# Routing of the last four token tiles at once, counts behind the first block, and destination columns rewritten in halves

## What is computed

```python
router_logits = x @ gate_w.T                         # 16 experts
topk_w, topk_idx = jax.lax.top_k(softmax(router_logits), 4)
topk_w = topk_w / topk_w.sum(axis=-1, keepdims=True)
shared = _silu_mul(x @ shared_gate_up.T, 704) @ shared_down.T
shared = shared * sigmoid(x @ shared_gate_vec.T)
# for each expert: acc + (silu_mul(x @ w_gu.T) @ w_d.T) * combine weight
return shared + sparse
```

## Time and profile before

| | before |
|---|---|
| runs, median (lowest to highest) | 738.39 us (736.25 to 744.0) |
| the profiled execution, device time | 739.09 us |
| its span | 737.3 us |
| TensorE busy | 560.7 us (76%) |
| VectorE busy | 492.3 us (67%) |
| GpSimd busy | 344.7 us (47%) |
| ScalarE busy | 285.3 us (39%) |
| indirect transfers of the dispatch (L1280), busy | 65.2 us in 64 |

### The profile page before, as it was taken

How to read it: one execution, slowest core, us unless ns; L and a number is a source line. 1 busy time by engine, 2 the same in 40 slices (tenths; PEclk the granted TensorE clock), 3 DMA queues, 4 the chain that set the end, 5 groups by cost and what they waited for, 6 DMA issues and landing times. The chain is left out here.

```text
span 737.3 us, 14872 instructions
## 1 busy us (share of the span) xinstructions
PE 560.7 (76%) x4194; PEld 483.8 (66%) x4195; DVE 492.3 (67%) x1202; ACT 285.3 (39%) x692; POOL 344.7 (47%) x420
## 2 busy tenths in 40 slices
PE   4268898899864998878388989950389999999900
PEld 1146677777753887767266868840289999999900
DVE  0567888889860648474848687540567777777758
ACT  1244445554532644334133434320344444444400
POOL 1026576677653446656610766672024444444410
PEclk9698999999985999999669999985599999999955
DMA  9121212221002755261132366535484444443177
GB/s 303 68 72 37 65 46 72 71 64 43 28 1 82 221 160 175 71 202 43 43 89 82 135 196 201 182 134 172 110 256 132 131 129 130 129 129 115 67 288 307
DMA packets 66122, 91.82 MB, mean 125 GB/s; under 512 B 8544, under 2 KB 56480, under 8 KB 66080
## 3 DMA queue, kind: packets, MB, share of 16 engines
q1 hardware_dynamic: 56144, 69.79, 31.4%
q0 software_dynamic: 6912, 19.01, 7.1%
q10 hardware_dynamic: 3024, 2.50, 1.0%
HBM read 53.23 MB, written 35.95 MB: 121 GB/s over the span
## 5 line engine op out<-in xcount | busy, mean ns | idle before, releaser
L1623 POOL DMA_INDIRECT results<-yb,xe x80 | 77.0, 962 | 109.6 <-DVE yb L1706 106.9
L1280 POOL DMA_INDIRECT dispatched<-rows,slot x64 | 65.2, 1019 | 46.5 <-DVE slot L1372 27.1
L1755 PE MATMUL bank<-wgu_hi,xT_hi 128*128 x160 | 60.1, 375 | 3.2 <-DVE xT_lo L1687 3.2
L1739 PE MATMUL bank<-ident,xe 128*128 128x128 f32 x160 | 32.0, 284 | 37.8 <-DMA xe<-dispatched 37.3
L1700 DVE TENSOR_TENSOR e_hT_lo<-bank,e_hT_hi 128x256 fp32r<-128x256 f32 x80 | 34.0, 425 | 32.2 <-ACT e_hT_hi L1656 32.2
L980 DVE TENSOR_TENSOR a_lo<-act,a_hi 128x512 fp32r<-128x512 f32 x32 | 28.3, 885 | 39.6 <-ACT a_hi L946 39.2
L1755 PE MATMUL bank<-wgu_lo,xT_hi 128*128 x160 | 52.6, 329 | 0.0
L1755 PE MATMUL bank<-wgu_hi,xT_lo 128*128 x160 | 52.5, 328 | 0.0
L435 POOL TENSOR_TENSOR orms<-omse,neghalf 128x16 f32<-128x16 f32 x16 | 46.7, 2921 | 1.7 <-POOL omse L432 0.8
L1739 PEld LDWEIGHTS bank<-ident,xe 128*128 128x128 f32 x160 | 19.9, 145 | 39.9 <-DMA xe<-dispatched 38.1
L542 DVE TENSOR_TENSOR probs<-bank,causal 128x512 f32<-128x512 f32 x64 | 42.1, 683 | 4.8 <-PE bank L677 4.4
(11 more groups left out here) (235 smaller groups left out, 1920.0 us busy)
## 6 DMA issues: line engine op xcount, KB each, us to landing
dispatched<-fill SPq DMA_DIRECT2D x20, 520.0 KB, 6.8
xe<-dispatched SPq DMA_DIRECT2D x80, 130.0 KB, 2.3
trig<-t_trig SPq DMA_DIRECT2D x16, 512.0 KB, 3.5
stage<-expert_gu SPq DMA_DIRECT2D x16, 352.0 KB, 3.5
wgu_hi<-results SPq DMA_DIRECT2D x11, 512.0 KB, 7.9
xt<-L_attn_x SPq DMA_DIRECT2D x32, 128.0 KB, 3.5
wgu_lo<-results SPq DMA_DIRECT2D x5, 512.0 KB, 16.5
x_rows<-h_all SPq DMA_DIRECT2D x16, 128.0 KB, 2.0
```

The costliest lines, as they stand in the source:

```text
L1280: pool.indirect_dma_start(out=dram["dispatched"], out_offset=bass.IndirectOffsetOnAxis(ap=slot[:, k, t:t + 1], axis=0), in_=rows[:, t, :], ...
L1623: pool.indirect_dma_start(out=dram["results"], out_offset=bass.IndirectOffsetOnAxis(ap=xe[:, r, E:E + 1].bitcast(INT), axis=0), in_=yb[:, ...
L1739: tr = nc.tensor.transpose(t_bank[r % 2][:, k * P:k * P + P], xe[:, r, k * P:k * P + P], ident[:, :])
L1755: mm = nc.tensor.matmul(gu_bank[p][:, 0:GU], xT[xn_][:, p, k, :], wgu[wn][:, k, e, :], start=(k == 0 and i == 0), stop=(k == KB - 1 and i ...
```

## The change

`choose` handles tiles 12 to 15 in one set of operations of four times the width, at the very start, with the still unused `x4` as scratch; only the running count is made tile by tile. SyncE therefore waits for the third step of the chain before it loads `x4`. `count` moves behind `first_product` of block 0, and `bases` and `slots(0)` behind VectorE's block 0; the other slots and the three `low_down` follow. GpSimd rewrites the destination column in two halves of eight tiles, each waiting only for its own eight transfers of the round before, and waits in round k for k + 1 slot vectors.

```diff
@@ GpSimd
+            def number(k, half):
+                for t in range(half * HALF, half * HALF + HALF):
+                    wait(pool, s_sent[t], 16 * k)
+                cols = slice(half * HALF, half * HALF + HALF)
+                nc.gpsimd.tensor_copy(rows[:, cols, E:E + 1].bitcast(INT), dest[:, k, cols].unsqueeze(2)).then_inc(S["col"], 1)
+            pool.wait_ge(S["tab_in"], 64)
+            number(0, 0)
+            number(0, 1)
             for k in range(TOPK):
-                for t in range(NT):
-                    wait(pool, s_sent[t], 16 * k)
...
-                nc.gpsimd.tensor_copy(rows[:, :, E:E + 1].bitcast(INT), dest[:, k, :].unsqueeze(2)).then_inc(S["col"], 1)
-                pool.wait_ge(S["col"], k + 1)
-                pool.wait_ge(S["slots"], TOPK)
-                for t in range(NT):
...
+                for half in range(2):
+                    if k:
+                        number(k, half)
+                    pool.wait_ge(S["col"], 2 * k + half + 1)
+                    pool.wait_ge(S["slots"], k + 1)
+                    for t in range(half * HALF, half * HALF + HALF):
@@ VectorE
-            choose(NT - 4)
-            low_down(0)
-            low_down(1)
+            choose()
...
                 if g == 0 and b == 0:
-                    choose(NT - 2)
-                    choose(NT - 1)
+                    bases()
+                    slots(0)
+                    low_down(0)
                 elif g == 0 and b == 1:
+                    low_down(1)
                     low_down(2)
-                    bases()
-                elif g == 0 and b in (2, 3):
-                    slots(2 * b - 4)
-                    slots(2 * b - 3)
+                    slots(1)
+                elif g == 0 and b == 2:
+                    slots(2)
+                elif g == 0 and b == 3:
+                    slots(3)
@@ SyncE
+                if first:
+                    sp.wait_ge(S["chain"], 3)
@@ TensorE
-                pe.wait_ge(S["chain"], 5 * TPG)
+                pe.wait_ge(S["chain"], 4 + TPG)
...
-                    if isinstance(g, int) and g == 0 and b == 2:
+                    if isinstance(g, int) and g == 0 and b == 0:
                         count()
```

More of the change, by code:

```diff
@@ L1175, in shared_and_dispatch @@
         later, ones = sh[:, 0, 0:P], sh[:, 0, P:2 * P]
-        versus = sh[:, 1, :].rearrange("p (e x) -> p e x", x=NX)
+        versus = x4[:, :, :].rearrange("p t (e x) -> p t e x", x=NX)
         steps, tile_no = sb("steps", [P, NX]), sb("tile_no", [P, ETILES])
@@ L1269, in _ @@
             pool.wait_ge(s_filled, 16 * (ETILES // 4))
-            for k in range(TOPK):
-                for t in range(NT):
-                    wait(pool, s_sent[t], 16 * k)
-                if k == 0:
-                    pool.wait_ge(S["tab_in"], 64)
-                nc.gpsimd.tensor_copy(rows[:, :, E:E + 1].bitcast(INT), dest[:, k, :].unsqueeze(2)).then_inc(S["col"], 1)
-                pool.wait_ge(S["col"], k + 1)
-                pool.wait_ge(S["slots"], TOPK)
-                for t in range(NT):
-                    pool.indirect_dma_start(out=dram["dispatched"], out_offset=bass.IndirectOffsetOnAxis(ap=slot[:, k, t:t + 1], axis=0),
-                                            in_=rows[:, t, :], in_offset=None).then_inc(s_sent[t], 16)
+            HALF = NT // 2
+            def number(k, half):
[6 more added lines that the diff above has]
+            number(0, 1)
+            for k in range(TOPK):
+                for half in range(2):
[4 more added lines that the diff above has]
+                    for t in range(half * HALF, half * HALF + HALF):
+                        pool.indirect_dma_start(out=dram["dispatched"], out_offset=bass.IndirectOffsetOnAxis(ap=slot[:, k, t:t + 1], axis=0),
+                                                in_=rows[:, t, :], in_offset=None).then_inc(s_sent[t], 16)
             for t in range(NT):
@@ L1341, in flat, with choose @@
                 return x[:, :, :].rearrange("p t e -> p (t e)")
[L1343 to L1349, removed]
-                chain(nc.vector.tensor_tensor(before_tile[:, t + 1, :], before_tile[:, t, :], chosen[:, t, :], ALU.add))
+            def choose():
+                last = slice(NT - TPG, NT)
+                chain(nc.vector.tensor_tensor(versus[:, :, :, :], logits[:, last, 0:NX].unsqueeze(2).broadcast_to([P, TPG, NX, NX]),
+                                              logits[:, last, 0:NX].unsqueeze(3).broadcast_to([P, TPG, NX, NX]), ALU.subtract))
+                chain(nc.vector.scalar_tensor_tensor(versus[:, :, :, :], ebefore[:, :, :].unsqueeze(1).broadcast_to([P, TPG, NX, NX]), -TINY,
+                                                     versus[:, :, :, :], ALU.mult, ALU.is_lt))
+                chain(nc.vector.tensor_reduce(order[:, last, :], versus[:, :, :, :], AX.X, ALU.add))
+                chain(nc.vector.tensor_scalar(chosen[:, last, :], order[:, last, :], TOPK - 0.5, None, ALU.is_lt))
+                for t in range(NT - TPG, NT):
+                    chain(nc.vector.tensor_tensor(before_tile[:, t + 1, :], before_tile[:, t, :], chosen[:, t, :], ALU.add))
+                return done[0]
             def bases():
@@ L1459, in body @@
                             add_shared(g - 1, i, 1 - q)
-                    if isinstance(g, int) and g == 0 and b == 0:
-                        choose(NT - 3)
                     hidden(g, b)
```

## The result

| | before | after |
|---|---|---|
| runs, median (lowest to highest) | 739.03 us (736.25 to 744.0) | 720.29 us (715.64 to 728.84) |
| runs | 4 | 4 |

The ratio is 0.9733, with a 95% interval of 0.969 to 0.9776: 18.7 us less, where 721.5 us had been predicted. Ratios and intervals, here and in the experiments, leave out executions more than 1.5% above the fastest of their kernel; medians are those of all. The execution whose trace is read here is the slowest of the four, 728.84 us: its work ahead of the changed stage took 8.9 us longer than before's (the stage starts at 384.44 instead of 375.54), so times are given from the stage's start, as "+101.5". A second profile of the same kernel, from the experiments (`e9_change_again`, 720.62 us, stage from 374.35), has no such delay and is read beside it.

The account below looks back on a forecast made before the run. The scatter chain was taken to end the shared stage some 18 us after the compute chain; with compute ending at 493.5, the next stage starts 17.8 us earlier: 739.09 - 17.8 = 721.3, given as 721.5, range 718 to 727.

Parts of the forecast that it names:

- What bounds the kernel: Between shared and expert stage: GpSimd's scatters and the load behind them end some 18 us after compute and its stores.
- The start of the scatter: GpSimd's first scatter, waiting only for slots(0) behind block 0, starts at 391.0, 15.2 us earlier than before.
- The turns: GpSimd's column rewrites between scatters: six of 2.0 us (1.5 to 3.0) replace three of 5.0; last issue at 478.5.
- The shared ports: Each of GpSimd's six column copies could lose 0.75 us to a VectorE instruction, 4.5 in all, without moving the sum.
- The slack: At the stage's end: expert_d lands at 490.0, 5.4 us before the scatter chain would decide the end.
- Rival 1: Scatter chain still ends the stage last; with every second turn at its old 5.0 us, 725 us; chance 0.12.
- The compute chain: The shared expert's blocks up to VectorE's last operation: 0.3 us late from the load wait, ending at 493.5.
- the walk: Step-by-step timing of the first blocks: first expert load there at 396.9, ScalarE's split 0.8 us, hid(2) at 398.6.
- The sum: The next stage begins at 496.9 instead of 514.76, 17.8 us earlier, with the expert stage unchanged: 721.3, given as 721.5.
- Rival 2: Late staging: each of the first four expert loads holds ScalarE and VectorE 1.4 us longer, 727 us; chance 0.10.
- Rival 3: Nothing gained, as the next stage waits for something else at its start: 738 us; chance 0.04.
- Rival 4: TensorE's clock stays at 1.2 GHz for part of the expert loop; fifteen tiles give 751 us; chance 0.04.

Follow-up runs that it names:

- e9_change_again: The changed kernel itself, nothing altered, timed once more in the second set: 722.15 us, ratio 0.9785.
- e6_before_two_rounds: The kernel before with two of its four rounds of scatters left out, the combine reading the other two twice: 723.01 us, ratio 0.9796.
- e3_change: The changed kernel itself, nothing altered, timed beside its variants on another occasion: 786.92 us, ratio 1.063.
- e11_short_rows: The changed kernel with 64 more scatters, of 16-byte rows into a tensor of their own, ahead of its own scatters: 800.34 us in a single run.
- e4_down_first: The changed kernel with the first two low_down calls back ahead of block 0, as before the change: 786.18 us, ratio 1.0617.
- first and third sets: Two of four groups of kernels timed together, on different chips; the change took 786.92 us in the first, the variant nearest to it 785.15 in the third.
- second and fourth sets: The other two groups of kernels timed together; the change took 722.15 us in the second, the variant nearest to it 727.45 in the fourth.
- e8: The changed kernel with GpSimd waiting, before each burst of eight scatters, until all earlier ones have landed: 736.03 us, ratio 0.9976.
- e12: The changed kernel with GpSimd waiting for all earlier scatters before each burst of eight, from the third round on only: 727.45 us, ratio 0.9857.
- e1_halves_only: The kernel before with GpSimd's column rewritten in halves alone, routing and wait for all four slot vectors as before: 786.59 us, ratio 1.0647.
- e4b_down_first: The kernel of e4_down_first timed again on another chip: 785.15 us, ratio 1.0607.

## Why the prediction was right, point by point

- **What bounds the kernel: right.** The scatter chain ended before's stage. `e6_before_two_rounds` shows it, and its floor of 121.0 us stands beside the +121.4 at which the prediction let the compute chain end the stage.
- **The start of the scatter: right.** Predicted 15.5 us after the stage's start, measured 14.8. The operations of 1,024 columns took 1.22 to 1.23 us as interpolated, and the Silu hid them: VectorE still waits 3.19 us for it. The 0.7 us less is ScalarE, whose first down-weight chunk was there at +4.7 instead of +5.5.
- **The turns: a little too long.** The three old turns of 5.0 were in truth 5.06, 3.73 and 6.02, the same in sum. Of the new ones six of 2.0 were predicted; measured were 1.68, 1.91, 1.54, 1.61, 1.96 and 1.44, together 10.1 instead of 12. With 1.34 to 1.35 a step inside bursts (predicted 1.324) the last issue came at +101.5; predicted +103.0.
- **The shared ports.** Of six copies three took longer than 0.21 us: 0.30, 0.36 and 0.73. Each of the three started while VectorE ran an operation with two SBUF inputs, and ended 0.05 us behind that operation's end: the one at 464.14, shown above, beside `s_a_lo` (464.13 to 464.82), the others with 0.25 and 0.31 us of theirs left (442.03 and 453.38). The other three found none, or one with 0.02 us left; `e9_change_again` shows the same pattern (0.31, 0.37, 0.72). So a copy loses what is left of the operation that it meets, which bears the rule of the Trainium skill (SBUF — State Buffer, reading the diagram) out. The 4.5 us that the prediction drew from it was the case in which every copy meets a whole one; the loss was 0.8 in all. That the scatters lose time in the same way is likely, not shown: with VectorE mostly silent, in `e3_change` and in the long rows of `e11_short_rows`, every copy took 0.20 to 0.22, and first to last scatter were 81.8 and 81.7 us instead of 86.8.
- **The slack: wrong.** "Last issue at 478.5, `expert_d` issued at 481.0": 2.5 us between them, taken from before. Measured 6.8 and 6.3. The term that was mis-sized is the landing of the last scatters: in before nothing else was under way when they landed; now they are issued 24 us earlier, and there SyncE's last expert load and its four `x4` loads are under way. The prediction had 5.4 us of slack; there is none. (By its own rows it was 4.3 from the start: the next stage began 11.57 us after the issue of `expert_d`, which from 481.0 gives 492.6 against the 496.9 of the sum.) That it cost 0.2 to 0.4 us and no more is luck of the size: the two chains came out level. Rival 1 (this chain still last) was therefore nearer than its 0.12 and came by a mechanism that it does not name; it had looked at turns, not at landing.
- **The compute chain: right within 1.5 us.** `hid(2)` at +21.8 and +21.7 (predicted +23.1), `hid(4)` at +29.3 (predicted +30.7, before +30.4), VectorE's end at +116.7 and +116.5 (predicted +118.0). VectorE waits for the first expert load's split as the walk says (1.75 us). Of the 1.3 us it is early, 0.7 is the earlier ScalarE and 0.5 the load, which ScalarE began to split 3.2 us after the end of `low_down(1)` (404.62 after 401.43) where 3.7 were taken. `e4_down_first` shows that VectorE's 1.75 us are the price of the moved `low_down`. TensorE's longest wait of the stage is 2.54 us for `low_down(0)` (its second product starts at +14.4, predicted +15.2).
- **The sum.** 19.2 and 19.5 us less for the stage, 17.8 predicted; expert stage 222.7 us, 222.5 predicted. Rival 2 (late staging) is out: no later load is waited for so long. Rival 3 is out by the result. Rival 4 is out: the expert stage shows tenths of 9 in its clock as before.
- **What was not thought of at all** is the slow issuing of the first and third sets. The prediction gave 0.04 to a loss, and by a mechanism in another stage. It holds in the measurement of the result and in the second and fourth sets; in the first set the change is 43 us slower than before, and in the third what is nearest to it is too. Its row in a trace is plain ("PE bank <- issue"), but no row of before pointed to it.

What stays open: what causes it. Known is that it needs an occasion (one chip had it and, ten minutes later, not), that on such an occasion the kernel before spreads too (735 to 765 us, against 735 to 751 in the other two sets), that it is much worse with the halves, and that it starts 10 to 18 us into unbroken scattering. Whether it is the making of addresses on GpSimd, its traffic, or a third party on the chip was not separated: `e8`, `e11` and `e12` all met clean occasions. Nor do the queues that bring instructions decide anything: in `e3_change` they moved nothing from 425 to 480, in `e1_halves_only` one block, with TensorE slow in both.

Two things set all seven traces of the first and third sets apart from the other seven, and the first is there long before this stage. The loads of the program's first stage (`xt<-L_attn_x`) landed after a median of 4.2 to 5.0 us, against 2.5 to 3.5. And the traces hold 7,350 to 7,740 semaphore records where the others hold 10,170 to 11,450 (`e3_change` 7,730, `e9_change_again` 10,411, of the same kernel), so that the profile has no landing time for the scatters there. Missing records can hide what ended a wait, though hardly within one product, as in the three matmuls shown, where no semaphore is waited for. Every execution on record carries a span and a granted clock from the profiler, so a disturbance of the recording itself is a rival that nothing here rules out.

## What to carry to other kernels

When two chains end a stage, the slack of the one behind must be worked out with the landing times of the place where it will then lie, not of the place where it lay: a scatter that lands after 2.5 us alone took 6.2 to 6.7 us beside the last loads of another queue. A pause that looks like pure loss (GpSimd waiting for its own transfers) may protect another engine, though that was not shown here: measure such a change on more than one occasion and more than one chip, and look for TensorE rows with "issue" as releaser. Here whole columns with the early routing lose an estimated 1 to 5 us where all is well and were 38 us faster than the change where it was not (29 us faster than `e4b_down_first` in the third set).

## What the runs showed of the hardware that was not expected

- In two of the four sets TensorE issued one matmul each 1.4 to 4.2 us instead of each 0.24 us, for some 55 us on end in `e3_change` (425 to 480, behind a milder stretch from 407), within one product and so with nothing to wait for, while GpSimd issued indirect scatters without a pause; the DMA engines were then 30% busy and moved 107 GB/s.
- Scatters of 128 rows took GpSimd 0.96 us at a median and follow each 1.27 us, whether a row has 16 or 1,040 bytes. With VectorE busy some take 1.2 to 1.6 us, and the 64 took 86.8 us from first to last; with it mostly silent they took 81.7 and 81.8.
- The landing of a scatter at the end of the stage depended on SyncE's loads beside it: 6.2 and 6.7 us when issued 0.2 to 0.3 us behind one expert load, 2.7 to 2.8 behind another and just ahead of four `x4` loads (`e9_change_again`, after), 2.4 to 2.6 us when issued 10 us or more after the last of them (`e12_late_bursts`, `e8_bursts_of_eight`). The Trainium skill (DMA: Bandwidth & Descriptors, "Issuing engines are not separate DMA queues") says that transfers of all issuing engines run on the same 16 engines and interleave; these rows agree.
